# The opening of the experts inside the drain of attention: whose engine makes the first low parts, and what TensorE does while attention ends

## The reference

```python
x = _layernorm(x + _L0_xattn_ref(x, ctx_2048, ...))
x = _layernorm(x + _L0_ffn_ref(x, w_router, wg, wu, wd, sg, su, sd))
...
logits = einsum('th,eh->te', xt, w_router)            # 8 experts
topk_w, topk_i = top_k(sigmoid(logits), 2)            # two of them, weights normed to sum 1
out  = sum over the two chosen e of weight * (silu(xt @ wg[e]) * (xt @ wu[e])) @ wd[e]    # 640 inner columns
out += sum over 2 shared experts of (silu(xt @ sg[j]) * (xt @ su[j])) @ sd[j]
```

## Time and profile before

| what | us | share of the span |
|---|---|---|
| median of 3 runs | 770.0 | |
| the profiled execution | 770.26 | |
| its span (15115 instructions) | 768.6 | 100% |
| TensorE (PE) busy | 706.3 | 92% |
| VectorE (DVE) busy | 563.7 | 73% |
| ScalarE (ACT) busy | 472.8 | 62% |
| GpSimd (POOL) busy | 350.2 | 46% |

### The profile page before, as it was taken

One profiled execution on the slowest core, in us unless ns is written; L12 is line 12 of the kernel. 1 busy time (PEld: TensorE's weight loads), 2 busy tenths in 40 slices (PEclk: granted clock), 3 DMA queues, 4 the chain that ended last, 5 costly groups with the idle time before them and its releaser, 6 DMA issues.

```text
span 768.6 us, 15115 instructions
## 1 busy us (share of the span) xinstructions
PE 706.3 (92%) x4958; PEld 640.7 (83%) x4958; DVE 563.7 (73%) x1174; ACT 472.8 (62%) x1066; POOL 350.2 (46%) x514
## 2 busy tenths in 40 slices
PE   4998888887999999999999996998999999999965
PEld 3888676676889999898999985877999999999855
DVE  4964688887878888888888885684778777776536
ACT  4444755447777777777777775353577776776401
POOL 0002566688998787878787775062000000000341
PEclk9999999999999999999999999899999999999978
DMA  9002400010200000000420030066376676660121
GB/s 296 4 1 81 174 1 1 1 34 28 63 8 2 7 0 7 0 7 0 140 71 0 0 104 1 3 245 215 117 234 197 229 252 198 223 220 29 56 68 56
DMA packets 45939, 64.81 MB, mean 84 GB/s; under 512 B 4288, under 2 KB 34880, under 8 KB 45632
## 3 DMA queue, kind: packets, MB, share of 16 engines
q1 hardware_dynamic: 40080, 56.45, 22.2%
q0 software_dynamic: 1536, 4.20, 1.7%
q10 hardware_dynamic: 4272, 3.51, 1.6%
HBM read 53.14 MB, written 11.01 MB: 83 GB/s over the span
## 4 chain that ended last, share of the span: by engine, by line
PE 61%; POOL 7%; DVE 4%; issue 4%; ACT 3%; another core or an unknown queue 1%; POOLq 0%; DVEq 0%; ACTq 0%
PE two L67 9%; PE two L69 7%; PE two L68 7%; PE bg L67 7%; PE bg L69 7%; PE bg L68 7%; PE bd L69 3%; PE bd L68 3%; PE bd L67 3%; PE two L321 3%; POOL under_dt L595 1%; PE two L296 1%; POOL under_raw L581 1%; POOL under_raw L576 1%
## 5 line engine op out<-in xcount | busy, mean ns | idle before, releaser
L1856 POOL DMA_INDIRECT gu_raw<-rows_out,slot x16 | 15.5, 971 | 201.3 <-DMA rows_out<-y_sb 196.7
L2002 ACT ACTIVATE sg<-bg 128x256 f32<-128x256 f32 (+1 forms) x95 | 40.7, 429 | 99.9 <-PE bg L69 89.5
L414 ACT ACTIVATE under_dt<-two,nb,under_raw 128x256 f32<-128x256 f32 x128 | 70.6, 562 | 44.8 <-DVE nb L497 44.8
L67 PE MATMUL bg<-xb_hi,gu_hi 128*128 128x256 f32 x300 | 86.2, 287 | 2.7 <-DVE xb_lo L2111 2.7
L69 PE MATMUL bg<-xb_hi,gu_lo 128*128 128x256 f32 x300 | 84.8, 283 | 0.0
L68 PE MATMUL bg<-xb_lo,gu_hi 128*128 128x256 f32 x300 | 84.8, 283 | 0.0
L2088 DVE TENSOR_TENSOR hf<-sg,bg 128x256 f32<-128x256 f32 (+1 forms) x95 | 45.0, 473 | 51.3 <-ACT sg L2002 49.2
L67 PE MATMUL two<-under_h 128*128 128x256 f32 (+1 forms) x208 | 66.9, 322 | 2.8 <-PEq L118 1.5
L68 PE MATMUL bd<-dn_lo,eh_hi 128*128 128x256 f32 x220 | 62.6, 285 | 3.4 <-issue 3.3
L69 PE MATMUL bd<-dn_hi,eh_lo 128*128 128x256 f32 x220 | 62.8, 286 | 2.1 <-issue 2.1
L595 POOL TENSOR_SCALAR under_dt<-under_dt,rec 128x256 f32<-128x256 f32 x128 | 62.3, 505 | 3.8 <-DVE rec L543 3.8
(11 more groups left out here) (292 smaller groups left out, 2532.9 us busy)
## 6 DMA issues: line engine op xcount, KB each, us to landing
gu_raw<-in_gu SPq DMA_DIRECT2D x17, 1280.0 KB
dn_raw<-in_dn SPq DMA_DIRECT2D x17, 640.0 KB
rows_in<-under_dt SPq DMA_DIRECT2D x1, 3840.0 KB, 13.1
rows_out<-y_sb SPq DMA_DIRECT2D x30, 128.0 KB, 2.1
x_blk<-rows_in ACTq DMA_DIRECT2D x13, 256.0 KB, 2.7
under_raw<-in_wq SPq DMA_DIRECT2D x1, 2048.0 KB, 8.0
under_raw<-in_wkv SPq DMA_DIRECT2D x1, 2048.0 KB, 12.6
under_raw<-in_wo SPq DMA_DIRECT2D x4, 512.0 KB, 4.0
```

Source lines behind the costliest of these rows:

```text
L67: pe.matmul(out, lh, rh, start=first, stop=False)
L414: act.activation(self.prob[:, g % 2, h, :], self.b_s[:, h // 2, (h % 2) * MW:(h % 2 + 1) * MW], ACT.Exp, bias=self.nb[:, h:h + 1], scale=s ...
L2002: act.activation(sg[:, u % 3, 0:width(u)], gate_of(u), ACT.Silu).then_inc(f_sg, 1)
```

## The change

GpSimd's two low parts become two VectorE operations inside the drain (`dve_weights`): one before `dve_o(N1)`, one before `dve_o(N3)`. The turns of x move into the drain: 0 and 1 after `pe_turn_p` of N2, and 2 after that of N3 (now in the bank `bg[1]`), with ScalarE's copies (`act_x`) behind its own steps there and VectorE's splits 0 and 1 after `dve_p(N2)`. Unit 0 is parted: its gate half stands before the last output product, its up half behind it, ahead of the logits. ScalarE's and VectorE's work on unit 0 moves ahead of the last copy of x and of the logits' use. Unit 2 is parted around `ranks`, so its gate half now stands ahead of them. VectorE's last split of x moves behind the places, the owners and the roundings of units 0 and 1; `owners` moves directly behind `hf` of unit 2. The functions `pe_turn_x`, `pe_logits` and `pe_unit` are the former local ones, but for what the diff shows.

```diff
@@ pe_tail
         self.pe_turn_p(pe, 2, N2, None)
+        self.ex.pe_turn_x(pe, self, 0)
+        self.ex.pe_turn_x(pe, self, 1)
         self.pe_out(pe, LAST, 1, N1)
         self.pe_values(pe, 2, N2)
         self.pe_turn_p(pe, 3, N3, None)
+        self.ex.pe_turn_x(pe, self, 2)
         self.pe_out(pe, LAST, 2, N2)
         self.pe_values(pe, 3, N3)
+        self.ex.pe_unit(pe, 0, 0, 0)
         self.pe_out(pe, LAST, 3, N3)
...
@@ act_tail
         self.act_p(act, N2)
+        self.ex.act_x(act, 0)
+        self.ex.act_x(act, 1)
         self.act_o(act, N2)
         self.act_p(act, N3)
+        self.ex.act_x(act, 2)
         self.act_o(act, N3)
...
@@ dve_tails
         self.dve_tail2(dve, LAST - 1)
+        self.ex.dve_weights(dve, 0)
         self.dve_o(dve, N1)
         self.dve_rec(dve, N3)
         self.dve_p(dve, N2)
+        self.ex.dve_x(dve, 0)
+        self.ex.dve_x(dve, 1)
         self.dve_o(dve, N2)
         self.dve_p(dve, N3)
+        self.ex.dve_weights(dve, 1)
         self.dve_o(dve, N3)
         self.dve_tail(dve, LAST)
-        self.ex.dve_x(dve, 0)
         self.dve_tail2(dve, LAST)
...
@@ pool_tail
             self.pool_step(pool, LAST, g, False, True)
-            if g >= 2:
-                self.ex.pool_weights(pool, g - 2)
...
+        turned = (bd[0], bd[1], bg[1], bx[1])
...
+        def pe_turn_x(pe, at, q):
+            pe.wait_ge(at.a_x2, 2 * q + 2)
+            if q == 0:
+                pe.wait_ge(at.a_exp, NS * AREP)
+            elif q == 2:
+                pe.wait_ge(at.a_klo, NS)
...
+        def pe_unit(pe, q, i, s):
...
+            if u == 0 and s == 1:
+                pe.wait_ge(r_f, 3)
...
@@ pe_program
-            turn_x(0)
-            turn_x(1)
-            turn_x(2)
-            pe.wait_ge(s_router, 32)
+            pe_unit(pe, 0, 0, 1)
             for b in range(4):
-                logits(b)
-            turn_x(3)
+                pe_logits(pe, b)
+            pe_turn_x(pe, at, 3)
             for b in range(4, BATCH):
-                logits(b)
+                pe_logits(pe, b)
             for q in range(NG_):
-                gate_up(q, 0)
+                if q:
+                    gate_up(q, 0)
                 gate_up(q, 1)
                 if q:
                     down(q - 1)
-                else:
-                    ranks()
                 if 2 <= q <= NBLK:
                     turn_block(q - 1)
-                gate_up(q, 2)
+                if q == 0:
+                    pe_unit(pe, 0, 2, 0)
+                    ranks()
+                    pe_unit(pe, 0, 2, 1)
+                else:
+                    gate_up(q, 2)
...
@@ act_program
+            act.wait_ge(at.a_x2, BATCH)
+            act.wait_ge(s_zero, 16)
+            gate(0)
+            act_x(act, 3)
             act.wait_ge(r_c, 1)
             act.activation(eneg[:, :, :], logit[:, :, :], ACT.Exp, scale=-1.0).then_inc(r_e, 1)
...
@@ dve_program
-            dve_x(dve, 1)
+            dve.wait_ge(s_zero, 16)
+            gated(0)
             dve_x(dve, 2)
             dve.wait_ge(r_l, 1)
...
-                if q == 0:
-                    dve_x(dve, 3)
                 gated(IT * q + 1)
                 if q == 0:

                     places()
                     gated(2)
+                    owners()
                 rest_h(IT * q)
+                if q == 0:
+                    gated(3)
...
                 rest_h(IT * q + 1)
                 if q == 0:
-                    owners()
+                    dve_x(dve, 3)
```

More of the change, by code:

```diff
@@ L1759, in experts @@
         flat_gu = lambda t: t[:, :, :, :].rearrange("p s k n -> p (s k n)")
+        turned = (bd[0], bd[1], bg[1], bx[1])
[5 more added lines that the diff above has]
+                pe.wait_ge(at.a_klo, NS)
+            for k in range(KT):
+                for b in range(2):
+                    mm = pe.transpose(turned[q][:, k * 256 + b * P:k * 256 + (b + 1) * P],
+                                      x_tok[:, 2 * q + b, k * P:(k + 1) * P], ident[:, :])
+            mm.then_inc(r_t, 1)
@@ new lines, in pe_logits @@
+        def pe_logits(pe, b):
+            if b == 0:
+                pe.wait_ge(s_router, 32)
+            pe.wait_ge(r_f, b // 2 + 1)
+            for k in range(KT):
+                mm = pe.matmul(bd[0][:, b * E:(b + 1) * E], x_f[:, k, b * P:(b + 1) * P], wr[:, k, :],
+                               start=(k == 0), stop=(k == KT - 1))
+            if b == BATCH - 1:
+                mm.then_inc(r_l, 1)
+        def pe_unit(pe, q, i, s):
+            u, w = IT * q + i, weights_of(q)
+            c, ws = w % 2, slice(i * P, (i + 1) * P)
+            if i == 0 and s == 0:
+                if q < 2:
+                    pe.wait_ge(r_lo, 2 * q + 2)
+                elif not shared(q):
+                    pe.wait_ge(f_xlo, q - 1)
+            if s == 0 and before_on_bank(u) >= 0:
+                pe.wait_ge(f_h, before_on_bank(u) + 1)
+            if u == 0 and s == 1:
+                pe.wait_ge(r_f, 3)
+            if i == 0:
+                pe.wait_ge(w_gl[c], 2 * (w // 2) + s + 1)
+            for k in range(KT):
+                if shared(q):
+                    tok = slice((q % 2) * HALF, (q % 2 + 1) * HALF) if q < 2 else \
+                        slice((q - NBLK - 2) * HALF, (q - NBLK - 1) * HALF)
+                    x2 = (x_hi[:, k, tok], x_lo[:, k, tok])
+                else:
+                    x2 = (xT_hi[q % 2][:, k, :], xT_lo[q % 2][:, k, :])
+                mm = products(pe, (gate_of(u), up_of(u))[s], (gu_hi[c][:, s, k, ws], gu_lo[c][:, s, k, ws]), x2,
+                              k == 0, k == KT - 1)
+            if s == 1:
+                mm.then_inc(f_g, 1)
@@ L1761, in load_first, with act_x @@
+        def act_x(act, q):
+            act.wait_ge(r_t, q + 1)
+            act.activation(x_f[:, :, q * 256:(q + 1) * 256], turned[q][:, :].rearrange("p (k t) -> p k t", k=KT),
+                           ACT.Copy).then_inc(r_f, 1)
         def load_first(sp):
@@ L1769, in act_weights, with dve_weights @@
             act.activation(gu_hi[0][:, s, :, :], gu_raw[0][:, s, :, :], ACT.Copy).then_inc(w_gh[0], 1)
[L1771 to L1774 removed]
+        def dve_weights(dve, s):
+            dve.wait_ge(w_gh[0], s + 1)
+            dve.tensor_tensor(gu_lo[0][:, s, :, :], gu_raw[0][:, s, :, :], gu_hi[0][:, s, :, :].bitcast(F32),
+                              ALU.subtract).then_inc(w_gl[0], 1)
         def dve_x(dve, q):
@@ L1867, in gate_up @@
             def gate_up(q, i):
[L1868 to L1888 removed]
+                pe_unit(pe, q, i, 0)
+                pe_unit(pe, q, i, 1)
             def down(q):
@@ L2045, in evict @@
                 act.activation(y_sb[n % 4][:, :], bd[s][:, 0:DM], ACT.Copy).then_inc(f_ye, 1)
-            turned = (bd[0], bd[1], bx[0], bx[1])
-            for q in range(4):
-                act.wait_ge(r_t, q + 1)
-                act.activation(x_f[:, :, q * 256:(q + 1) * 256], turned[q][:, :].rearrange("p (k t) -> p k t", k=KT),
-                               ACT.Copy).then_inc(r_f, 1)
+            act.wait_ge(at.a_x2, BATCH)
+            act.wait_ge(s_zero, 16)
+            gate(0)
+            act_x(act, 3)
             act.wait_ge(r_c, 1)
@@ L2057, in act_program @@
                     round_h(IT * q - 1)
-                gate(IT * q)
+                if q:
+                    gate(IT * q)
                 gate(IT * q + 1)
@@ L2247, in dve_program @@
                     rest_h(IT * q - 1)
-                gated(IT * q)
+                if q:
+                    gated(IT * q)
                 if last:
@@ L2281, in dve_program @@
                         norm_stats(b)
-                gated(IT * q + 3)
+                if q:
+                    gated(IT * q + 3)
                 rest_h(IT * q + 2)
```

54 lines of the change are left out of this document (5 added, 49 removed).

## The result

The changed kernel takes 767.81 us (median of 11 runs, 765.58 to 770.01) against 772.61 us for the kernel before, measured again in 11 runs (769.99 to 777.15): a ratio of 0.9943, 95% interval [0.9926, 0.9961]. The forecast was 766.7 us, the range 763.3 to 770.5. The kernel before is the less steady one: of its first three runs, whose median is the 770.0 us at the start, two are the lowest of the eleven.

The account below looks back on a forecast made before the run. TensorE was taken to bound the kernel, with gains only in attention's drain and the experts' opening. Terms -1.70 - 1.38 - 0.45 = -3.53 us took 770.26 to 766.7 us (chance 0.50), range 763.3 to 770.5.

Parts of the forecast that it names:

- GpSimd's low parts: Attention's drain: moved to VectorE, they no longer hold up `nb`, so the chain to TensorE shortens: -1.70 us.
- Turns and first unit in the drain: Attention's drain: turns of x and half of unit 0 fit TensorE's gaps of 3.12, 0.54 and 1.41 us: 0.
- Products ahead of the ranks: Experts' opening: 18 products instead of 24 between logits and ranks, at the full clock: -1.38 us.
- The clock: Experts' opening: loss from the low clock shrinks with the stretch of turns and tiny products, 2.38 to 1.93: -0.45 us.
- rival (a): Experts' opening: the clock does not fall, another 1.75 us off: 765.0 us; chance 0.17.
- After the ranks: Up to the sixth unit: VectorE's last split of x takes back 1.38 us: 0 gain, about 1.3 us TensorE idle.
- ScalarE's tables: Experts' opening: two added table loads, 1.28 us each by the row, stay hidden: 0, with 0.5 us to spare.
- the sum with a further drain: Experts' opening: 1283 ns plus about 1380 ns per table switch would make the copy some 0.9 us late.
- The scatter: Sixteen indirect stores after the ranks: they begin 0.8 us earlier against TensorE's program; the 2.7 us stall stays: 0.
- Rival (b): First expert's down products: the stall beside the indirect transfers grows by 5.5 us: 772.3 us; chance 0.09.
- Rival (c): Attention's drain: VectorE's splits of x and GpSimd's scaling delay each other, +1.1: 767.8 us; chance 0.12.
- Rival (d): Attention's drain: the 1.86 us `nb` has another cause and stays, so the -1.70 falls away: 768.4 us; chance 0.12.

Follow-up runs that it names:

- e5: The changed kernel again, unedited, in series 2: 0.9910 of the kernel before.
- e10: The changed kernel again, unedited, in series 3: 0.9900 of the kernel before, median 769.71 us.
- e1: The kernel before, with only the two low parts of the first weights moved from GpSimd to VectorE: 0.9923 of the kernel before.
- e2: The changed kernel with the two low parts back on GpSimd: 0.9953 of the kernel before.
- e11: The changed kernel with all of unit 0, and ScalarE's and VectorE's work on it, back behind the logits: 0.9949 of the kernel before.
- e9: The same kernel as e1, run again in series 3: 0.9934 of the kernel before, median 771.99 us.
- e3: The changed kernel with VectorE's last split of x right behind the owners, ahead of two roundings: 0.9866 of the kernel before.
- series 2: Runs of e5, the before-kernel with spare products in the drain, e7 and e8, on one chip with the kernel before (median 773.03 us).
- series 3: The runs of e9 to e12 on one chip, with their own runs of the kernel before (median 776.53 us).
- e4: The changed kernel with the second block's weights loaded behind the first two loads of rows: 0.9884 of the kernel before.
- e8: e3 plus 8 and 4 spare products around the first turn of sent rows: 0.9895 of the kernel before, without one execution of 3841.64 us.
- e12: e8 plus e4's order of loads: 0.9858 of the kernel before, median 765.78 us, without one execution of 2390.02 us.
- e7: The changed kernel with 12 spare products on TensorE between the eighth and ninth unit, beside the stores: 0.9915 of the kernel before.

## Why the prediction was right

The time lay in the range, 1.1 us over the forecast in the median, and the sum of 3.53 us is what the profile shows at the end of the span (303.3 to 299.8). Both are partly luck. The sum started from an execution of 770.26 us, 2.35 under the median that the kernel before then took, and the medians lie 4.80 us apart, 1.27 more than the sum; the two differences leave 1.1. At the end of the span e5 and e10 gained 3.0 and 2.9 us, and that mark moves by 2 us from profile to profile for other reasons. The terms did not all come as said.

*GpSimd's low parts*, -1.70: measured 1.70 at the exponentials, and shown as their cause by e1 and e2. VectorE's own two (1.48 us each) cost nothing; the gaps they stand in shrank from 1.80 and 2.37 to 0.34 and 0.99 us.

*Turns and first unit in the drain*, 0: right, with 0.06 us to spare ahead of the first output product. The cover that the first unit gives to the last norm was missed as a gain (e11).

*Products ahead of the ranks*, -1.38: 1.51 between e1 and the changed kernel, both with the clock up. The choice met them within 0.1 us, as said.

*The clock*, -0.45: this is the step that failed. The sum took a fall of the clock in the opening as given and its loss to go by the length of the stretch of turns and tiny products. In the profiled execution the clock was 1.00 there, which the prediction had named as a sign of being wrong: the loss was not 1.93 us but 0, and the logits themselves ran 1.1 us faster (3.94 us from their start to the first product behind them, 5.04 before), which the sum had left out. So the ranks came 6.33 us earlier, not 3.53. That was rival (a), which would have given 765.0, and it came in seven of the eight profiles of this opening. In e5, the eighth, the prediction's picture holds: the 18 products took 6.33 us, 2.00 more than in the changed kernel's first profile (4.33), and the ranks came 3.31 us earlier than before.

But in the profiled execution the clock fell behind the stores instead: 1.65 us more from the sixth unit to the first turn, 1.53 from there to the third. In e5, where it fell in the opening and TensorE idled the same 3.11 us beside the stores, those are 0.2 and 0.0. So the clock cost about 3 us at one place or the other, and the right total rests partly on two errors that cancel. What makes it fall where it does stays open: e1 and e9 (one program, two openings), and the changed kernel's three profiles show that it is no property of the instructions alone. The Trainium skill, "TensorE: Matmul & The Clock Gate", section "Part 1: The HAM clock gate", says that the chip's look at the engine runs freely and doesn't start with the kernel; these profiles are in line with that, but none of them shows it.

*After the ranks*, 0 gain and 1.3 us idle: 0.28 lost and 0.95 idle. The last split of x was the wait, as said; with it moved up, the third turn in e3's profile is 3.2 us earlier (2.0 beside e10's), for a reason that wasn't foreseen, but no run shows what that edit alone is worth in time.

*ScalarE's tables*, 0 with 0.5 us to spare: 0 with 0.2. A load takes 1.28 us and the next activation follows at once (483.54 to 484.84); the last copy of x is over at 486.25 and the next load starts at 486.27. So the sum with a further drain, which the prediction gave beside its own, is not what this trace shows.

*The scatter*, 0: 0.2 by e5. Rival (b), which put 5.5 us there, did not come. Rival (c), contention beside the splits, is there but small: `x_lo` takes 0.84 us beside GpSimd's scaling and 0.69 otherwise, the scaling 2.01 against 1.84. Here the Trainium skill's rule on VectorE and GpSimd ("SBUF — State Buffer", "Who interferes with whom") agrees with the trace, as it does with `nb`. Rival (d) is refuted by e1.

The other comparisons came out larger, 0.990 and 0.991. Part of it is the clock. An estimate of what it costs a kernel is the span times one less its mean granted clock, averaged over the runs (at most, since a fall while TensorE idles costs nothing). In series 2 that is 15.2 us for the 17 runs of the kernel before and 12.4 for the six of e5, 2.8 of the 6.5 us between their mean spans; in series 3 it is 19.3 for the kernel before and 13.4 for e10, 5.9 of 7.9 us, and 14.1 for e9, which could account for all of its 5.0 us. So the runs don't separate what the shorter chain is worth from what the clock gives. The profiled execution of before, on which the sum was built, was one of its quickest.

## What to carry to other kernels

A small operation that takes ten times its usual length is worth a look at what GpSimd does in the same microseconds: 0.16 against 1.86 us here, and by the medians taking GpSimd's operation away was two thirds of this change (0.66% of 1.00% in series 3, with intervals that overlap and the clock in both). A fall of the clock that one profile shows is not a fixed cost of the code beneath it: take a second profile of the same kernel before putting a price on it. And what a chain gains can be lost again further on (6.3 us at the ranks, 2.9 three blocks later, most of the difference by the clock), so follow a gain through marks counted from a common event.

## What was not expected

Beside the indirect stores engines see results late: ScalarE took the eighth unit 4.6 us after TensorE's last product of it (520.62 against about 516.0), although the DMA engines were only 0.40 busy from 518 to 524 us. Leaving half of the loads for later (e4) changed nothing in that; a split of x that starts 2.0 us earlier against the row maxima (e3, e8, e12) made it go away in each of three profiles. The stores themselves stretch beside VectorE's operations on two tiles: one takes 2.29 us at 502.18 in the changed kernel, where VectorE makes a low part that starts just ahead of it (502.16, 1.48 us); so it is in e5, e7 and e11. In e2, e4 and e10 the same two start within 0.02 us of each other as well, yet the store takes 0.96 us and the low part 1.54. In e10:

```profile
501.51 1.54 DVE L2132 TENSOR_TENSOR dn_lo<-dn_raw,dn_hi 128x1280 fp32r<-128x1280 f32 x1
...
501.52 0.96 POOL L1913 DMA_INDIRECT rows_in<-x_tok,slot  x1 [0.30 <-issue]
```

What decides between the two is not shown.
